# A decoder layer with two-of-eight experts: rows turned by DMA instead of TensorE, and a reordered end

## The reference

```python
x = layernorm(x + attention(x))              # 16 heads of 16, causal
x = layernorm(x + (x @ gelu(ctx @ L).T) @ ctx)   # ctx has 1601 rows
shared   = silu(x @ W1s.T) @ W2s.T               # hidden width 1024
top2     = top_k(x @ gate_w.T, 2); g = softmax(top2)   # 8 experts
selected = sum over the 2 chosen experts of g_e * (silu(x @ W1e.T) @ W2e.T)
x = layernorm(x + shared + selected)
```

## Time and profile before

| | |
|---|---|
| median of 3 runs | 860.20 us |
| the profiled execution, its time | 859.96 us |
| its span in the trace | 858.1 us |
| PE busy, share of the span | 808.3 us, 94% |
| DVE, ACT, POOL busy | 66%, 62%, 35% |
| `finish` | from 475 us to the end |

### The profile page before, as it was taken

The page is one execution under the profiler, slowest core; times in us unless marked ns, Lnnn a source line. Parts: engine busy times, 40 slices in busy tenths (PEclk is TensorE's granted clock), DMA queues, the critical chain, the costliest instruction groups (busy, mean ns, idle before and its releaser), DMA issues. The chain is left out here.

```text
span 858.1 us, 19630 instructions
## 1 busy us (share of the span) xinstructions
PE 808.3 (94%) x7444; PEld 498.1 (58%) x7445; DVE 563.4 (66%) x1037; ACT 534.8 (62%) x797; POOL 297.5 (35%) x207
## 2 busy tenths in 40 slices
PE   4899999999999999999998798999999999999994
PEld 1367333333333333333332686889999999877883
DVE  4575789999999999999950685853333333322366
ACT  4341778777788778777788576545444444434555
POOL 5040693444442434444440100032333333211133
PEclk9999999999999999999999996999999999999997
DMA  8683244333434444434121896011111111100243
GB/s 290 119 217 149 111 149 149 109 107 113 138 130 149 149 149 149 122 107 178 61 92 73 328 420 234 2 50 39 51 49 46 46 49 48 45 20 26 70 144 101
DMA packets 37224, 102.41 MB, mean 119 GB/s; under 512 B 7325, under 2 KB 20830, under 8 KB 32798
## 3 DMA queue, kind: packets, MB, share of 16 engines
q1 hardware_dynamic: 32814, 90.60, 31.6%
q0 software_dynamic: 4000, 10.36, 3.8%
q10 hardware_dynamic: 336, 0.40, 0.4%
HBM read 65.55 MB, written 32.37 MB: 114 GB/s over the span
## 5 line engine op out<-in xcount | busy, mean ns | idle before, releaser
L169 DVE TENSOR_REDUCE partial<-ring 128x1 f32<-128x512 f32 (+3 forms) x509 | 308.7, 669 | 30.2 <-PE ring L151 21.4
L690 ACT ACTIVATE probs<-scores 128x1024 f32<-128x1024 f32 (+1 forms) x320 | 270.9, 904 | 62.7 <-PE scores L737 31.9
L753 PE MATMUL acc<-probs,values 128*32 128x512 f32 (+3 forms) x1280 | 170.1, 541 | 0.9 <-ACT acc_sb L695 0.7
L1337 PE MATMUL turned<-mats,weights 128*128 128x256 f16 (+1 forms) x1488 | 160.1, 263 | 2.5 <-DVE mats L1585 1.5
L1361 PE MATMUL ops<-weights,work 128*128 (+1 forms) x1320 | 150.7, 274 | 6.2 <-DVE res L1611 5.0
L1180 ACT ACTIVATE hid<-turned 128x512 f32<-128x512 f32 (+1 forms) x112 | 65.7, 586 | 145.4 <-PE turned L1337 131.1
L1337 PEld LDWEIGHTS turned<-mats,weights 128*128 (+1 forms) x1488 | 136.4, 98 | 22.9 <-issue 4.1
L151 PE MATMUL ring<-kstack,qstack 48*128 48x512 f16 (+1 forms) x580 | 144.0, 350 | 2.2
L1361 PEld LDWEIGHTS ops<-weights,work 128*128 128x128 f16 x1320 | 129.1, 98 | 23.6 <-DVE res L1611 5.3
L1593 DVE TENSOR_TENSOR work<-hid,work 128x512 f16<-128x512 f32 (+1 forms) x112 | 76.1, 682 | 100.7 <-ACT work L1185 100.7
L665 POOL TENSOR_TENSOR a_w_in<-a_w_in,w_scale 128x2304 f32<-128x2304 f32 x16 | 64.4, 4027 | 206.7 <-DMA a_w_in<-w_all 206.7
(11 more groups left out here) (195 smaller groups left out, 762.6 us busy)
## 6 DMA issues: line engine op xcount, KB each, us to landing
...
weights<-w_split_d SPq DMA_DIRECT2D x9, 2048.0 KB, 26.5
...
attn<-by_token SPq DMA_DIRECT2D x16, 256.0 KB, 3.9
...
res<-x SPq DMA_DIRECT2D x1, 2048.0 KB, 9.2
```

The lines of the kernel that those rows point to most:

```text
L169: return nc.vector.tensor_reduce(out=found[:, places[0]:places[-1] + 1:step], in_=bank[:, 0:WIDTH[n]].rearrange("p (k w) -> p k w", k=len( ...
L690: nc.scalar.activation(probs[:, s % 2, at:at + w], scores[half][:, first:first + w], ACT.Exp, scale=QK_SCALE).then_inc(exp_done, 1)
L753: mm = nc.tensor.matmul(acc[VW * j:VW * (j + 1), QB - w:QB], values[:, h, k0 + j], probs[:, s % 2, at:at + w], start=first, stop=last)
L1337: mm = nc.tensor.matmul(hps[b][:, j * TW + first_row:j * TW + first_row + w], weights[:, a, bass.ds(at + (k * HID + (b * HB + j) * P), P)] ...
```

## The change

**Rows are turned by DMA.** ACT and (for six of eight chunks) POOL split the normalised rows into float16 halves `x16`, and SP turns each chunk of 256 rows (both halves, 256 KB) by one DMA transpose into `allT`. Steps 0 to 2 and the gates' product read `allT`; for the steps after that SP issues a DMA transpose each, from gathered rows (`x_rows`, now float16 halves) into `xT`. `turn`, `first_half_x` and `second_half_x` are gone; items 8 to 11 too. The logits are six times four matmuls of 32 x 512 with four column groups of PE, copied to SBUF and turned back by four transposes, in the middle of `widen(1)`.

**Weights.** `x16` and `allT` lie where the weights of experts 7 and 6 go. SP loads the shared expert and five others first; POOL issues the other three after the transposes: expert 5 when all eight are in, 7 when `rows_d` is stored, 6 when the third `widen` is done. PE waits for them before step 3.

**Order.** `rank_tokens` moves behind `narrow(0)`; on DVE the second halves of steps 0 and 1 move in front of and around the placing.

**End.** `returned` holds all eight chunks, where experts' weights were. SP issues its loads after the last transpose. ACT scales both results, POOL adds them to each other, DVE adds the sum to `res`; the deviation is a power of -0.5 on POOL for each chunk, and ACT finishes chunks 0 to 3 already in step 26. The last step's second tile has a bank of its own.

The core of the diff:

```diff
 
-    rows_d = nc.dram_tensor("rows_d", (S, D), f32).ap()
...
-        xT = mats[:].bitcast(f16).rearrange("p (i s c n) -> p i s c n", i=2, s=2, c=DC)
+        xT = mats[:].bitcast(f16).rearrange("p (i g s c n) -> p i g s c n", i=2, g=TB, s=2, c=DC)
...
+        returned = weights[:, 0, 0:NC * 2 * TB * D * 2].bitcast(f32).rearrange("p (c r t d) -> p c r t d", c=NC, r=2, t=TB)
+
+
+
+        x16 = weights[:, :, (NE - 1) * WE:NE * WE].rearrange("p a (t s d) -> p a t s d", s=2, d=D)
+        allT = weights[:, :, (NE - 2) * WE:(NE - 1) * WE].rearrange("p a (t s c n) -> p a t s c n", s=2, c=DC, n=P)
...
+        f_stats_done, f_aggr_done, f_var_done, f_nmean_done, f_rstd_done, f_shift_done = (
+            sem("f_stats_done"), sem("f_aggr_done"), sem("f_var_done"), sem("f_nmean_done"), sem("f_rstd_done"), sem("f_shift_done"))
+        act_final, dve_final, stored = sem("act_final"), sem("dve_final"), sem("stored")
+        SCALED_IN = {F0: (0, 1), F0 + 1: (2, 3, 4, 5), F0 + 2: (6, 7)}
+        COMBINED_IN = {F0 + 1: (0, 1, 2, 3), F0 + 2: (4, 5, 6, 7)}
+        LATE = 2
+        FINAL_AHEAD = 4
...
+        def halves_of_rows(first_tile, tiles):
+
+            a, t = divmod(first_tile, NT // 2)
+            return (x16[:, a, t:t + tiles].rearrange("p t s d -> p (t s d)"),
+                    allT[:, a, t:t + tiles].rearrange("p t s c n -> p (t s c) n"))
+
...
+        def second_halves_of_rows(engine, n):
+            a, t = divmod(n * TB, NT // 2)
+            return engine.tensor_tensor(x16[:, a, t:t + TB, 1], res[:, n * TB:(n + 1) * TB], x16[:, a, t:t + TB, 0], ALU.subtract)
+
+        def load_expert(queue, e, signal):
+            queue.dma_start(weights[:, :, e * WE:(e + 1) * WE],
+                            w_split_d[:, :, e * WE:(e + 1) * WE].rearrange("a p w -> p a w")).then_inc(signal, 16)
...
-            for e in range(NE):
-                sp.dma_start(weights[:, :, e * WE:(e + 1) * WE],
-                             w_split_d[:, :, e * WE:(e + 1) * WE].rearrange("a p w -> p a w")).then_inc(routed_in, 16)
+            for e in range(LOADED_FIRST):
+                load_expert(sp, e, routed_in)
+            for n in range(NC):
+                if n < LAST_HALVES:
+                    sp.wait_ge(x16_lo, n + 1)
+                else:
+                    sp.wait_ge(x16_lo_last, n - LAST_HALVES + 1)
+                rows, turned_rows = halves_of_rows(n * TB, TB)
+                sp.dma_start_transpose(turned_rows, rows).then_inc(allT_in[n], 16)
+
+            def turned_into(parity):
+                return xT[:, parity].rearrange("p g s c n -> p (g s c) n")
+
+            sp.wait_ge(product, NM)
+            for n in range(FROM_ALL, HEAD):
+                if n >= FROM_ALL + 2:
+                    sp.wait_ge(h_ready, (n - 1) * NB)
+                sp.dma_start_transpose(turned_into(n % 2), halves_of_rows(n * TB, TB)[0]).then_inc(xT_in[n % 2], 16)
+
...
-                sp.wait_ge(ln_done, NQ + g + 1)
...
-                             res[:, g * TPQ:(g + 1) * TPQ]).then_inc(rows_saved, 16)
+                             x16[:, a, t:t + TPQ].rearrange("p t s d -> p t (s d)")).then_inc(rows_saved, 16)
...
+            def step(n, parity):
+                count = groups(n)
+                if shared(n) is None:
+                    sp.wait_ge(rows_in[parity], rows_before(n, parity, 16 * TB) + 16 * count)
+                else:
+                    sp.wait_ge(own_rows_in[parity], (n - F0) // 2 * 16 + 16)
+                sp.wait_ge(h_ready, (n - 1) * NB)
+                sp.dma_start_transpose(xT[:, parity, 0:count].rearrange("p g s c n -> p (g s c) n"),
+                                       x_rows[:, parity, 0:count * 2 * D]).then_inc(xT_in[parity], 16)
+                if n + 2 >= F0 and n + 2 < NALL:
+                    t = shared(n + 2)
+                    sp.wait_ge(xT_in[parity], xT_count(n, parity))
+                    sp.dma_start(x_rows[:, parity].rearrange("p (t d) -> p t d", t=TB),
+                                 rows_d[t * TW:(t + 1) * TW, :].rearrange("(t p) d -> p t d", p=P)).then_inc(own_rows_in[parity], 16)
+
+            for n in range(R0, NALL):
+                step(n, n % 2)
...
-                if c >= NG:
-                    sp.wait_ge(combined, TB * (c - NG + 1))
...
-                    sp.dma_start(returned[:, c % NG, r],
+                    sp.dma_start(returned[:, c, r],
...
+            for c in range(NC - 1):
+                sp.wait_ge(act_final, TB * (c + 1))
...
+            for n in range(LAST_HALVES):
+                pool.wait_ge(x16_hi, n + 1)
+                second_halves_of_rows(nc.gpsimd, n).then_inc(x16_lo, 1)
+            pool.wait_ge(allT_in[NC - 1], 16)
+            for e in range(LOADED_FIRST, NE - 2):
+                load_expert(nc.gpsimd, e, late_in)
+            for n in range(FROM_ALL, HEAD):
+                pool.wait_ge(xT_in[n % 2], xT_count(n, n % 2))
+            pool.wait_ge(rows_saved, 16 * NQ)
+            load_expert(nc.gpsimd, NE - 1, late_in)
+            pool.wait_ge(gates_ready, 1)
+            pool.wait_ge(h_ready, FROM_ALL * NB)
+            load_expert(nc.gpsimd, NE - 2, late_in)
...
+            def find_scale(part, first_tile, last_tile):
+                tiles = slice(first_tile, last_tile)
+                pool.wait_ge(f_var_done, part + 1)
+                nc.gpsimd.tensor_tensor(f_rstd[:, tiles], f_veps[:, tiles], minus_half[:].broadcast_to([P, last_tile - first_tile]),
+                                        ALU.pow).then_inc(f_rstd_done, 1)
+                if part < NC - 1:
+                    pool.wait_ge(f_rstd_done, part + 1)
+                    pool.wait_ge(f_nmean_done, part + 1)
+                    nc.gpsimd.tensor_tensor(f_shift[:, tiles], f_nmean[:, tiles], f_rstd[:, tiles], ALU.mult).then_inc(f_shift_done, 1)
...
-                pool.wait_ge(scaled, TB * (c + 1))
-                if c < NC - 2:
-                    pool.wait_ge(y_done, y_count(c if c < HEAD else c - HEAD + F0, TB - 1))
-                tiles = slice(c * TB, (c + 1) * TB)
-                nc.gpsimd.tensor_tensor(res[:, tiles], res[:, tiles], returned[:, c % NG, 1], ALU.add).then_inc(pair_added, 1)
...
+                pool.wait_ge(scaled, 2 * TB * (c + 1))
+                nc.gpsimd.tensor_tensor(returned[:, c, 0], returned[:, c, 0], returned[:, c, 1], ALU.add).then_inc(pair_added, 1)
+                if c >= 2:
+                    find_scale(c - 2, (c - 2) * TB, (c - 1) * TB)
+            find_scale(NC - 2, (NC - 2) * TB, (NC - 1) * TB)
+            for i in range(TB):
...
+            def first_halves(g):
+                act.wait_ge(ln_done, NQ + g + 1)
+                for n in range(g * 2, g * 2 + 2):
+                    a, t = divmod(n * TB, NT // 2)
+                    nc.scalar.activation(x16[:, a, t:t + TB, 0], res[:, n * TB:(n + 1) * TB], ACT.Copy).then_inc(x16_hi, 1)
...
-            def scale_second(c):
-                act.wait_ge(returned_in[c % NG], 32 * (c // NG + 1))
-                for t in range(TB):
-                    tile = c * TB + t
-                    nc.scalar.activation(returned[:, c % NG, 1, t], returned[:, c % NG, 1, t], ACT.Copy,
-                                         scale=gates[:, 1, tile:tile + 1]).then_inc(scaled, 1)
...
+            def scale(c):
+                act.wait_ge(returned_in[c], 32)
+                for r in range(2):
+                    for t in range(TB):
+                        tile = c * TB + t
+                        nc.scalar.activation(returned[:, c, r, t], returned[:, c, r, t], ACT.Copy,
+                                             scale=gates[:, r, tile:tile + 1]).then_inc(scaled, 1)
...
+                        scale(c)
+                if isinstance(n, int) and n == F0 + 2:
+                    for c in range(FINAL_AHEAD):
+                        final(c)
...
+            def multiply_gates():
+
+                pe.wait_ge(added, NM)
+                for n in range(NC):
+                    pe.wait_ge(allT_in[n], 16)
+                m = 0
+                for k in range(DC):
+                    for a, b in products:
+                        for g in range(NQ):
+                            half, t = divmod(g * TPQ, NT // 2)
+                            mm = nc.tensor.matmul(gates_ps[VW * g:VW * (g + 1), :].rearrange("p (t n) -> p t n", t=TPQ),
+                                                  gate_split[:, b, k], allT[:, half, t:t + TPQ, a, k],
+                                                  start=(m == 0), stop=(m == 5))
+                        m += 1
+                mm.then_inc(gates_ready, 1)
+
+            def turn_logits():
+                pe.wait_ge(gates_copied, 1)
+                for t in range(TPQ):
+                    mm = nc.tensor.transpose(logits_ps[:, t * P:(t + 1) * P], turned_logits[:, t * P:(t + 1) * P], ident32[:])
+                mm.then_inc(logits_turned, 1)
...
-                pe.wait_ge(x_lo, n + 1)
+                if isinstance(n, int) and n < FROM_ALL:
```

(54 more changed lines are left out.)

241 lines of the change are left out of this document (98 added, 143 removed).

## The result

The changed kernel takes **853.57 us** (median, 852.19 to 854.55), the kernel before beside it 859.62 us (858.17 to 860.52): ratio 0.9929, 95% interval 0.9915 to 0.9942, so 6.05 us or 0.7% faster. Forecast were 844.0 us and a range of 836 to 866. Sign and range held; the gain is 6 us where 16 were forecast. The profiled execution took 854.55 us with a span of 852.4 us, where the forecast had a span of 841.8.

The account below looks back on a forecast made before the run. PE's own work was taken to bound the routed steps, DVE's routing chain the way there, DVE and ACT the end. Span 858.1 - 9.0 - 2.9 - 4.4 = 841.8 us, plus 1.9 around it, gave 844 us, range 836 to 866.

Parts of the forecast that it names:

- The end: From the last routed `narrow` to the end of the span: 47.6 us instead of 52.0, 4.4 us gained.
- T0: The end of the last routed `narrow`, from which the prediction counts times at the end; 806.1 us in the kernel before.
- The stores end 3.6 us on: At the end of the span: stores finish 3.6 us after DVE's last tile at T0 + 44, giving 47.6 us.
- Rival 3: At the end: nothing gained, as ACT scales twice as much and DVE and POOL slow each other; 848 us; chance 0.08.
- The steps: First routed `widen` to T0: 20.5 transposes of 0.44 us leave PE's path, 9.0 us gained.
- rival 4: In the steps: `widen` reads its rows in two pieces of 128 and loses some 10%; 856 us; chance 0.04.
- nothing else becomes late: In the steps: removing PE's transposes delays nothing else, so the whole 9.0 us is gained.
- The way to the steps: Items and routing ahead of the first routed `widen`: `widen(4)` starts at 565.4 instead of 568.26, 2.9 us gained.
- rival 1: Ahead of the steps: transposes at 3 to 4 us each hold the gates back; 852 to 860 us; chance 0.20.
- rival 2: Ahead of the steps: transposes go a descriptor at a time, 8.5 us each; 899 us; chance 0.18.
- Weights: Before the routed steps: three loads wait for the last transpose, the last in by 549; costs nothing, PE needs them at 565.

Follow-up runs that it names:

- late_by_act: Changed kernel with the scale of the last three parts found by Sqrt on ACT and reciprocal and shift on DVE, instead of POOL: 848.08 us, ratio 0.9869.
- before_late_pool: Kernel before the change plus one small POOL memset that waits for DVE's last tile and that nothing reads: 862.27 us, ratio 1.0034.
- read_ahead: Changed kernel with the returned rows of the first four chunks issued on SP ahead of the last transpose of rows: 848.33 us, ratio 0.9875.
- moments_by_pool: Changed kernel with variance plus eps and the negated mean of the final LayerNorm on POOL instead of DVE: 850.87 us, ratio 0.9908.
- joined_moments: joined with variance plus eps and the negated mean of chunks 0 to 5 on POOL: 841.43 us, ratio 0.9781.
- joined: Changed kernel with last scales on ACT and DVE, weight-column registers kept, returned rows read ahead and second halves on DVE: 840.30 us, ratio 0.9781.
- joined_old_end: Changed kernel with registers kept, returned rows read ahead and second halves on DVE, but the end of the kernel before: 842.96 us, ratio 0.9811.
- halves_by_dve: Changed kernel with the second halves of chunks 0 to 5 on DVE between the items, in place of POOL: 851.09 us, ratio 0.991.
- weights_meanwhile: Changed kernel with the weights of experts 4 and 5 loaded on POOL's queue while the rows are turned: 870.01 us, ratio 1.0117.

## Why the prediction was right in sign and wrong in size

**The end, forecast -4.4, measured +3.1: the step that failed.** In the sum DVE wrote its last tile at T0 + 44, with 3.6 us behind it; measured are 48.6 and 6.5. Two of the three errors have a run that gives their size.
- The stores were taken as the end ("The stores end 3.6 us on"). That was so before only because POOL's last operation lay 7.6 us ahead of the span's end. I moved a small operation of POOL to the very end, costed its 0.4 us (measured 0.72), and not that POOL's block then ends 6.7 us later. Worth 3.7 us (late_by_act; the converse in before_late_pool).
- The last transpose ahead of the returned loads was seen and named, with chunk 0 at T0 + 10.7. Measured are 13.0: SP issues 1.4 us after `widen(25)`, and the loads of chunk 0 take 6.4 us, not the 3.9 of the earlier trace rows. The order was taken as given, and what it costs wasn't asked: moving it away was worth 3.9 us (read_ahead). The chunks behind it weren't the limit, as they landed 1.4 us apart where I had 2.4 (2.5 by the sum's own figures).
- DVE was summed with durations from rows where POOL was idle. Beside POOL's sums the small addition takes 1.03 to 1.08 us three times and 0.60 once before the last `narrow`, not 0.16. Rival 3 had the cause, with the pair of 1.89 and 0.74 us in the earlier trace rows (two different operations, so no price of like against like), but priced it at 4 us in all, with ACT's doubled scaling, and gave it a chance of 0.08. What it is worth at the end isn't shown: without the small operations (moments_by_pool, joined_moments) the end is no shorter than the traces vary.

With the first two mended the end is 47.6 us (joined). That this is the forecast's number is luck: DVE's last tile comes at T0 + 45.1, not 44, and 2.4 us stand behind it, not 3.6. joined_old_end shows that the division of work was worth 2 to 3 us by then. The idea of the step was sound and its surroundings were not.

**The steps, forecast -9.0, measured -7.0.** The 16 whole steps did nearly what was forecast, 16 x 0.44 = 7.0: from `widen(4)` to `widen(20)` 174.7 us became 168.1, 5.24 + 5.24 each, at the clock 1.00 of the stretch 570 to 740, so rival 4 is out. The half steps gave nothing: from `widen(20)` to `widen(24)` 54.7 against 54.8 us. My sentence "nothing else becomes late" left out PE's own register loads: gaps of 0.24 to 0.28 us behind a transpose became 0.65. PE's gaps in that piece add up to 1.9 us before and 3.7 after, and the sequencer's records have a register load (`TENSOR_LOAD`, mostly 0.30 us) in or just ahead of each of them (742.88 to 743.19 at the gap from 743.09, for one). So by the gaps 1.8 of the missing 2 us are that; by the two runs with registers kept it is about 1.

**The way to the steps, forecast -2.9, measured -2.9: right for partly wrong reasons.** The transposes took 3.1 to 4.2 us to landing (4 taken) and 1.2 to 2.0 us of SP each (2 taken); the gates' product took 1.5 us, not 3.2. But the last normalisation ended at 520.0, 44.0 us after the function's start where 41.1 was forecast, in part since POOL's halves hold DVE (halves_by_dve gives 1.0 us of it back), and PE did two banks of `widen` in 4.45 us instead of 2.6, at the granted clock 0.50 from 520 to 526, having stood for 6.95 us. Counted from the span's start, `choose` came 3.1 us later than forecast, the list 1.5, and `widen(4)` 1.0, which is the late start alone; the cheaper product, gap and fetch made up for the rest. That the two -2.9 agree is partly luck.

**Rivals 1 and 2, 0.38 together**, are out for this kernel: eight transposes landed by 526.1, and the gates' product behind them started at 527.6, between the 522 and the 533 named as signs, held by the bank of `widen` ahead of it, which had waited for ACT. (The estimate of 10.5 us a chunk belongs to rival 2; the prediction calls it the third.) The chance wasn't wasted, though. weights_meanwhile shows the mechanism of rival 1 as soon as two loads run alongside. I had the wait for the last transpose down as free (right: PE never waited for weights), but did not say what it buys: 16 us. The Trainium skill (VectorE: DVE Perf Modes, The three transpose paths) gives 1309 ns for a 128x128 block; eight blocks in 3.3 us are 0.41 each, so taken one after another that figure isn't borne out here. The 261 GB/s of the Trainium skill (DMA: Bandwidth & Descriptors, Latency and other measured facts) is a rate, an estimate of 1.0 us for 256 KB: as such the trace bears it out, since the first two transposes landed 0.95 us apart (510.77 and 511.72), but it isn't the time to landing, 3.1 and more. For that my 4 us, from the nearest row, was the better guide.

**Weights** weren't waited for, as forecast, though the last load landed at 555.0 where I had 549.
